# Four gate buffers, gates kept in one piece per group, the last routing among the shared experts, and the last norm in two halves

## The reference

```python
x = layernorm(x + attention(x))            # 16 heads of 8 features
xf = x.reshape(-1, 128)                    # 2048 tokens
shared = (silu(xf @ sw1) * (xf @ sw3)) @ sw2          # hidden size 256
s = sigmoid(xf @ router_w.T)                          # 8 experts
_, topk_idx = top_k(s + router_bias, 2)
gates = s_sel / (s_sel.sum() + 1e-9)                  # comb: (tokens, 8), zero where not picked
h = gelu(einsum('nd,edh->neh', xf, ew1))              # every expert on every token
routed = einsum('ned,ne->nd', einsum('neh,ehd->ned', h, ew2), comb)
out = layernorm(x + shared + routed)
```

## Time and profile before

| | us |
|---|---|
| median of 3 runs | 259.37 |
| lowest and highest run | 257.46, 260.01 |
| the profiled execution, its own time | 260.36 |
| its span, first to last instruction | 258.0 |
| PE busy | 225.7 (87%) |
| DVE busy | 169.1 (66%) |
| ACT busy | 136.0 (53%) |
| POOL busy | 92.6 (36%) |

### The profile page before, as it was taken

One profiled execution on the slowest core, in us unless ns is written; L12 is line 12 of the kernel. 1 busy time (PEld: TensorE's weight loads), 2 busy tenths in 40 slices (PEclk: granted clock), 3 DMA queues, 4 the chain that ended last, 5 costly groups with the idle time before them and its releaser, 6 DMA issues.

```text
span 258.0 us, 4343 instructions
## 1 busy us (share of the span) xinstructions
PE 225.7 (87%) x1514; PEld 153.3 (59%) x1514; DVE 169.1 (66%) x352; ACT 136.0 (53%) x260; POOL 92.6 (36%) x172
## 2 busy tenths in 40 slices
PE   1975973999999999996599999999789999999970
PEld 1533843767767776774467766648566665666630
DVE  8953992777978979797239983136646564562853
ACT  2351711676776667665146678886585334434320
POOL 8678381000100106221236976543525632020201
PEclk9997996899999999999759999999999999999997
DMA  7277764404729074285100000009995089396111
GB/s 194 55 92 93 82 68 104 43 9 79 57 44 83 14 91 39 54 76 198 38 0 0 8 0 9 1 23 158 140 225 113 21 155 146 88 148 140 41 41 41
DMA packets 16196, 19.41 MB, mean 75 GB/s; under 512 B 1280, under 2 KB 11712, under 8 KB 16032
## 3 DMA queue, kind: packets, MB, share of 16 engines
q1 hardware_dynamic: 15744, 18.49, 43.6%
q0 software_dynamic: 144, 0.39, 1.0%
q10 hardware_dynamic: 288, 0.27, 0.5%
HBM read 11.22 MB, written 1.11 MB: 48 GB/s over the span
## 4 chain that ended last, share of the span: by engine, by line
PE 78%; DMA 7%; DVE 7%; issue 3%; ACT 1%; POOL 1%; SPq 1%; POOLq 0%; DVEq 0%
PE ring L811 18%; PE pv_bank L825 14%; PE max_bank L797 12%; PE max_bank L935 11%; DMA qstack<-top_rows 5%; DVE kstack L621 3%; PE ring L781 3%; PE ring L783 2%; PE ring L782 2%; DMA kstack<-qk_parts 2%; PE max_bank L783 2%; PE max_bank L781 2%; PE max_bank L782 2%; PE misc_bank L864 1%; PE misc_bank L875 1%
## 5 line engine op out<-in xcount | busy, mean ns | idle before, releaser
L661 DVE TENSOR_REDUCE top<-max_bank 128x2 f32<-128x512 f32 x128 | 84.0, 685 | 34.0 <-PE max_bank L797 32.8
L563 ACT ACTIVATE probs_mem<-ring 128x512 f32<-128x512 f32 x128 | 73.9, 597 | 45.6 <-PE ring L811 44.3
L811 PE MATMUL ring<-qstack,kstack 128*128 128x256 f32 x256 | 63.0, 331 | 9.7 <-DMA qstack<-top_rows 9.7
L811 PEld LDWEIGHTS ring<-qstack,kstack 128*128 128x128 f32 x256 | 40.6, 199 | 37.9 <-ACT probs_mem L563 25.1
L797 PE MATMUL max_bank<-kstack,qstack 128*128 128x256 f32 x256 | 55.3, 305 | 3.8 <-DMA kstack<-qk_parts 3.0
L797 PEld LDWEIGHTS max_bank<-kstack,qstack 128*128 128x128 f32 x256 | 41.9, 203 | 7.9 <-DMA kstack<-qk_parts 3.8
L825 PE MATMUL pv_bank<-probs_mem,v 128*18 128x256 f32 x512 | 41.3, 397 | 0.0
L732 DVE TENSOR_TENSOR probs_mem<-probs_mem,kstack 128x512 f32<-128x512 f32 x32 | 22.0, 691 | 22.9 <-ACT probs_mem L601 17.4
L935 PE MATMUL max_bank<-probs_mem,wf 128*128 128x512 f32 x64 | 32.4, 593 | 0.0
L601 ACT ACTIVATE probs_mem<-ring 128x512 f32<-128x512 f32 x21 | 12.5, 596 | 20.9 <-PE ring L783 19.3
L470 POOL TENSOR_SCALAR rstd<-mv 128x2 f32<-128x2 f32 x8 | 1.8, 224 | 51.1 <-DVE mv L698 51.0
(11 more groups left out here) (139 smaller groups left out, 336.3 us busy)
## 6 DMA issues: line engine op xcount, KB each, us to landing
kstack<-gate_scratch SPq DMA_DIRECT2D x4, 2048.0 KB, 15.8
kstack<-qk_parts SPq DMA_DIRECT2D x24, 64.0 KB
wf<-w_ffn_dram SPq DMA_DIRECT2D x1, 1408.0 KB, 5.7
qstack<-qk_parts SPq DMA_DIRECT2D x9, 128.0 KB
xs<-x_dram SPq DMA_DIRECT2D x4, 256.0 KB, 4.8
out_dram<-xs SPq DMA_DIRECT2D x4, 256.0 KB, 2.3
kstack<-wf_hi SPq DMA_DIRECT2D x12, 64.0 KB
qstack<-wf_hi SPq DMA_DIRECT2D x6, 128.0 KB
```

Of the source, the lines that this page charges most:

```text
L563: nc.scalar.activation(probs[:, k // 2 % 4, c % 2 * 512:(c % 2 + 1) * 512], ring[k % NRING][:, :], ACT.Exp, scale=SCALE).then_inc(probs_ma ...
L661: dve.tensor_reduce(top[:, half, h:h + 3:2], max_bank[n % NMAX][:, :].rearrange("p (h k) -> p h k", h=2), AX.X, ALU.max).then_inc(max_take ...
L811: ins = mm(ring[k % NRING][:, j * S:(j + 1) * S], kstack[:, s, ab, r, kt * P:(kt + 1) * P], qstack[:, s, r, :], start=True, stop=True)
```

## The change

Four edits. The gates of a group lie in one piece in device memory, and a load takes 16 KB in one run for each partition in place of eight runs of 2 KB. There are four gate buffers, the two new ones in the memory of `qstack`, which the attention no longer needs by then; the loads are placed at ticks `UP0` + 1, 2, 6 and 14, and that of group 2 or 3 waits for no expert any more. The router of group 3 stands at tick `UP0` + 6 in place of `EX0` = `UP0` + 8, and the steps behind it come one half tick apart in place of two; the gate transposes of group 2 stand at `UP0` + 4 in place of `EX0` + 1, those of group 3 at `UP0` + 13 (= `EX0` + 5) in place of `EX0` + 16. The end of the last group is done in two halves of 256 tokens, the second half's transposes in a bank of their own.

```diff
-        gate_dram = nc.dram_tensor("gate_scratch", (NE, TOK), F32, kind="Internal").ap()
+        gate_dram = nc.dram_tensor("gate_scratch", (NG, NE, GT), F32, kind="Internal").ap()
...
-        gates = [kstack[:, 2 + i, :, :, :].rearrange("p a r q -> p (a r q)").rearrange("p (e t) -> p e t", e=NE).bitcast(F32)
-                 for i in range(2)]
+        gates = [kstack[:, 2 + i, :, :, :].rearrange("p a r q -> p (a r q)").bitcast(F32) for i in range(2)]
+        gates += [qstack[:, 2 * i:2 * i + 2, :, :].rearrange("p s r q -> p (s r q)").bitcast(F32) for i in range(2)]
...
-            router = 2 * EX0 if late else 2 * first + (9 if b < 2 else 8)
+            router = 2 * (UP0 + 6) if late else 2 * first + (9 if b < 2 else 8)
...
-                    n = router + n * (2 if late else 1)
+                    n = router + n
...
-                comb_tick = {NG - 1: EX0 + 16, NG - 2: EX0 + 1}.get(b // 2, router // 2 + 7)
+                comb_tick = {NG - 1: UP0 + 13, NG - 2: UP0 + 4}.get(b // 2, router // 2 + 7)
...
+        FIN = [(g, 0, TPG) for g in range(NG - 1)] + [(NG - 1, t, t + TPG // 2) for t in (0, TPG // 2)]
         for g in range(NG):
-            jobs[max(UP0 + 1, EX0 + NE * (g - 1)), 1].append(("load gates", g))
+            jobs[UP0 + (1, 2, 6, 14)[g], 1].append(("load gates", g))
...
                 for kind, i in (("accT", 0), ("finT", 1), ("rstd2", 2), ("norm2", 7)):
-                    jobs[EX0 + m + LAG + 1 + i, 0].append((kind, g))
+                    for f, (group, t0, t1) in enumerate(FIN):
+                        if group == g:
+                            jobs[EX0 + m + LAG + 1 + i, 0].append((kind, f))
...
-                if g < 2:
-                    sp.wait_ge(scores_made, 4 * NSTEP)
-                else:
-                    sp.wait_ge(hid_made, NG * NSH + NE * (g - 1))
+                sp.wait_ge(scores_made, 4 * NSTEP)
                 for i in range(2):
                     sp.wait_ge(gate_stored[i], 16 * (g + 1))
-                src = gate_dram.rearrange("(o e) t -> o e t", o=1)[:, :, tokens(g)]
-                sp.dma_start(gates[g % 2], src.to_broadcast([P, NE, GT])).then_inc(gates_loaded[g % 2], 16)
+                src = gate_dram.rearrange("(o g) e t -> o g (e t)", o=1)[:, g, :]
+                sp.dma_start(gates[g], src.to_broadcast([P, NE * GT])).then_inc(gates_loaded[g], 16)
...
-                            dve.wait_ge(gates_loaded[m // NE % 2], 16 * (m // NE // 2 + 1))
+                            dve.wait_ge(gates_loaded[m // NE], 16)
...
                     if kind == "finT":
+                        g, t0, t1 = FIN[b]
                         pe.wait_ge(acc_taken, b + 1)
-                        if b:
-                            pe.wait_ge(fin_stats, b)
-                        for t in range(TPG):
-                            ins = nc.tensor.transpose(pv_bank[:, t * P:(t + 1) * P], acc_t[:, t * P:(t + 1) * P], ident[:, :])
+                        if g and t0 == 0:
+                            pe.wait_ge(fin_stats, g)
+                        for t in range(t0, t1):
+                            ins = nc.tensor.transpose(fin_bank(b)[:, t * P:(t + 1) * P], acc_t[:, t * P:(t + 1) * P], ident[:, :])
                         ins.then_inc(fin_made, 1)
```

More of the change, by code:

```diff
@@ L179, in build_layer @@
         route_dve, route_pool = sem("route_dve"), sem("route_pool")
-        gate_stored, gates_loaded = (
-            [sem(f"{n}{i}") for i in range(2)] for n in ("gate_stored", "gates_loaded"))
+        gate_stored = [sem(f"gate_stored{i}") for i in range(2)]
+        gates_loaded = [sem(f"gates_loaded{g}") for g in range(NG)]
         rw_split, w_hi_made, w_split = sem("rw_split"), sem("w_hi_made"), sem("w_split")
@@ L747, in _ @@
                     if kind == "norm2":
+                        g, t0, t1 = FIN[b]
                         dve.wait_ge(fin_rstd, b + 1)
[L749 to L750 removed]
+                        for t in range(t0, t1):
+                            ins = dve.tensor_scalar(xs[:, g * TPG + t, :], res2[:, t, :], mv2[:, t, 0:1],
                                                     rstd2[:, t:t + 1], ALU.subtract, ALU.mult)
```

43 lines of the change are left out of this document (25 added, 18 removed).

## The result

The median of four runs of the kernel after is 264.44 us (263.81 to 265.03), against 259.69 us (257.46 to 261.88) for four runs of the kernel before. The ratio is 1.0212, with a 95% interval of 1.0138 to 1.0285. Each ratio here leaves out the runs that count as slow, over 1.5% above the fastest of their kernel (above: 261.88), so it is not the ratio of the two medians, and routing_only, with one run left, has none. The profiled execution took 265.03 us, and its span is 263.3 us; before it was 260.36 and 258.0.

A forecast was written before the change was run, and what follows sets the result against it. From 195 us on, every TensorE instruction and every wait it feels lengthens the run. The terms +5.9 - 0.52 - 0.25 - 0.6 = +4.5 against the median 259.37 gave 263.9 us; 8-in-10 range 260.9 to 268.

The forecast's parts named there:

- First wait: TensorE waits ahead of expert 1 for VectorE's product of shared part 7, queued behind `sig`: +1.96 us.
- The chain: Group 3's routing on GpSimd, from `sel` to the last comparison: 6.9 us, 5.2 plus four VectorE instructions at 0.42.
- short enough: Rival: GpSimd runs at its free durations beside idle VectorE, gates there at 202.4, sum +2.2, 261.6 us; chance 0.2.
- Last steps: Group 3's routing behind `rank`: `mask` and `picked` 0.71 us, `den` to GpSimd's last steps 0.69, those 2.25; gates at 204.65.
- All three waits together: Product of expert 3 starts at 205.8 us, before at 199.96: +5.9, including the wait ahead of expert 1.
- the second: VectorE idles at `rank` until GpSimd's comparisons end at 200.5 us; the product of expert 2 comes only at 201.7.
- the third: TensorE waits 2 to 3 us at group 3's gate transposes, until 204.7, for GpSimd's last step.
- The clock: Rival: TensorE's granted clock falls at the new gaps; total 267.2 us if at the first, 268.4 at the last; chance 0.14.
- Groups 1 and 2: Expert stage: group 3's gate transposes leave group 1, -0.52 us; the gate-load wait goes, -0.25; both groups of equal length.
- Transposes of group 2: Gate transposes moved ahead of shared part 4, into TensorE's wait for VectorE: cost nothing, at most 0.3 us.
- Last norm: End of the last group in halves: -0.45 us, half-size store 0 to 0.4, in all -0.6, bounds -0.3 and -1.1.

The follow-up runs named there:

- routing_only: The kernel before with only the moved routing and gate transposes; 265.98 us, beside 260.27 for before on that chip.
- after_again: The kernel after, unchanged, measured once more beside more runs of the kernel before; 264.26 us, ratio to before 1.0249.
- clock_fill: The kernel after with products of no use in TensorE's two long gaps, ahead of expert 1 and group 3's gate transposes; 262.79 us, ratio to before 1.0131.
- last_wait_late: The kernel after with only group 3's gate transposes three ticks later, and their load behind them; 261.68 us, ratio to before 1.0136.
- first_wait_only: The kernel after, router still early, but steps from `rank` on and group 3's gate transposes as late as before; 260.29 us, ratio to before 0.9974.
- piece_only: The kernel before with only the one-piece layout of the gates in device memory, still two buffers; 260.38 us, ratio to before 1.0045.
- routing_back: The kernel after with group 3's routing and gate transposes back at their old places; 256.87 us, ratio to before 0.9869.
- back_fill: routing_back with five products of no use ahead of the shift waits of sequences 0 and 4, bank wait moved ahead of them; 251.95 us, ratio to before 0.9648.
- back_whole_norm: routing_back with the last norm undivided; 258.43 us, ratio to before 0.9983.

## Why the prediction was right, and where its sizes were off

Forecast were +4.5 us, from 259.37 to 263.9; measured were +4.75, from 259.69 to 264.44, and +4.67 between the profiled executions. The mechanism of the waits was right. That the sums agree so closely is luck: in the stretch that the change touches it cost +6.23, 1.7 more than forecast, mainly because the clock fell, and the forecast had that at nothing. It had named a fall between 191 and 205 us as a sign of being wrong, and by that sign it was. Stages that the change does not touch (-0.93) and the time outside the span (-0.63) brought the total back, and by the medians taken beside after_again it is only +3.2. Point by point, counted from the anchor:

- *First wait.* Forecast +1.7 at `down` of expert 0 (197.0 in place of 195.29). Measured +1.74 in clock_fill and +1.74 in routing_only. Table loads, the low part of shared part 5 on POOL, `sig`, and the product of shared part 7 follow one another as the prediction put it, and `sig` is there 8.71 after the anchor (forecast 8.68). ScalarE's exponential starts 187.80, the load started 186.51 and took 1.28: the drain of some 1380 ns that the Trainium skill has on "ScalarE: Activation LUTs", section on what ACT_TABLE_LOAD costs, does not appear, so the 2.8 us that it would have added did not come.
- *The chain.* Forecast 6.9 from `sel` to the last comparison, measured 6.85. The Trainium skill, "SBUF — State Buffer", section on who interferes with whom, lets VectorE instructions with two SBUF inputs hold up GpSimd. The rows agree with it in kind: the first comparison (four instructions, L493) took 2.38 us, beside three such instructions of DVE and the start of a fourth, and 1.04 us in group 2, where DVE was idle:

```profile
163.76 1.04 POOL L485 TENSOR_TENSOR diff<-sel 128x64 f32<-128x64 f32 x4
```

  The next step, beside the rest of the fourth, took 1.19 us in place of 0.86. Behind it DVE idles, and the last three steps take 0.85, 1.15 and 0.74 us, in group 2 0.86, 1.16 and 0.73. The excess of the first two is 1.67 us, the 4 x 0.42 of the forecast. That DVE's work is what stretched them was not isolated by a run of its own. The rival *short enough* (gates at 202.4) is refuted: the chain took 6.85 in place of 5.2.
- *Last steps.* From the end of `rank` to that of `picked` 1.09, forecast 0.71; from `den_ok` to the end 2.43, forecast 2.25. `mask` took 0.66 us; the product of expert 2 runs beside it on DVE. The prediction had this only as a bound ("`mask` held up by the product of expert 2"). The gates are there 204.22 - 183.53 = 20.69 after the anchor, forecast 204.65 - 184.46 = 20.19.
- *All three waits together.* Forecast +5.9 at `down` of expert 3, the first wait in it, measured +6.4 with the clock held (clock_fill). The 0.5 are those of the last steps. Separately, the second is 1.28 at the product behind `rank`, the third 2.60 at the transposes (last_wait_late removes only the latter).
- *The clock.* This is the step that failed. The forecast had no fall; the rival gave it 0.14, with a total of 267.2 or 268.4. It fell twice, behind 3.01 us ahead of expert 1 and behind 2.60 us ahead of the transposes, and cost 1.6 to 1.7 us (clock_fill against after: 1.65 by the first medians, 1.60 anchored, 1.70 at expert 4). So the rival came true in kind, and its size was wrong: I took the 9 us of low clock at 126 to 135 as the length of a fall, and each of these lasted some 3 us. The first of them cost nothing, since its 1.4 us ended in the wait for POOL's chain; where that wait is taken away, in first_wait_only, they count.
- *Groups 1 and 2.* `down` of the first expert of groups 1 to 3 starts so:

```profile
216.31 1.02 PE L948 MATMUL max_bank<-probs_mem,wf 128*128 128x512 f32 x2
...
230.58 1.02 PE L948 MATMUL max_bank<-probs_mem,wf 128*128 128x512 f32 x2
...
244.84 1.02 PE L948 MATMUL max_bank<-probs_mem,wf 128*128 128x512 f32 x2
```

  14.27 and 14.26 us, of equal length as forecast (before 14.70 and 14.43). From expert 4's product to the last one it is 0.71 less than before; forecast 0.52 + 0.25 = 0.77. "I give the one-piece layout nothing" beside "the gate buffers no longer wait for each other: -0.25" put the right gain to the wrong edit: piece_only shows that the layout alone brings it, and routing_only that the earlier transposes alone do.
- *Transposes of group 2.* Costed at nothing ahead of shared part 4, and nothing is what they show: before, PE waits 0.51 us for DVE there, and in the kernel after part 4 starts 2.81 us ahead of the anchor, before 2.80. What their leaving brings is seen at the start of the expert stage in routing_back, where `down` of expert 0 comes 0.57 us earlier than before; in the kernel after it is inside the +1.74.
- *Last norm.* Forecast -0.6 (bounds -0.3 and -1.1), measured -1.06 to -1.18 within the span and about -0.5 outside it. The step that was off is "1.02 us for each half": POOL's power of two columns takes 0.70, and the store's gain was put at 0 to 0.4. The norm ends 260.91 - 255.79 = 5.12 us after the last product, forecast 5.5.

The sum of what was measured: 6.42 (waits) + 1.70 (clock) - 0.71 (groups) - 1.18 (end) = +6.23 within the stretch. With -0.63 outside the span and -0.93 from unchanged stages, whose length differs between executions, that makes +4.67. Against the forecast the clock is +1.7 and the last steps +0.5; the end is -0.6 and the time outside the span -0.6, and the stages ahead -0.9.

The sign hung on whether PE has enough other work while the moved routing runs, and there the forecast was right. A tick of the shared experts is six products of 0.23 us, some 1.4 us, and one of the experts 1.55, where the routing of earlier groups had ticks of some 4 us. The kernel routing_back shows that the rest of the change alone is faster than before, by 1.81 us anchored and 1.3% by its ratio.

## What to carry to other kernels

Moving a serial chain of small steps earlier pays only if the stage it moves into is long enough to cover it; count the chain's length (here some 12 us from `sig` to the gates) against the consumer's distance in the new order, and count every in-order queue that now stands behind one of its steps. Change one thing at a time where several edits are independent: here three edits worth -1.8 us together were hidden by a fourth of some +8 us. And try products of no use in a gap of TensorE that cannot be avoided: in clock_fill and at sequence 0 of back_fill the wait took about as long as before, but what followed it ran at the full clock. Find the place of the gap by counting, in the trace, the instructions ahead of it: in back_fill the second five products missed theirs by one sequence.

## What the runs showed of the hardware that was not expected

- The granted clock is not decided by the length of one gap alone. It fell behind 0.65 us of idle time in piece_only (0.57 in 192 to 196 us), and did not fall behind 3.01 us in last_wait_late (1.00 in 192 to 200 us) and in routing_only, where it then fell behind the next gap, of 2.62 us. The kernels after (both times) and first_wait_only fell behind the same 3.01. The kernel before kept 1.00 behind the same 0.65 us. What decides between them stays open; all fell to half clock for about 3 us, where the earlier trace rows show some 9. The Trainium skill, "TensorE: Matmul & The Clock Gate", section on the clock gate, has it that an idle engine falls to half clock, and that the moment of a switch varies from run to run of the same kernel. The falls agree with the first, and the one gap of 3.01 us with and without a fall behind it with the second.
- The time of an unchanged kernel goes with its granted clock. Among the 23 executions of before on the chip of after_again, the shortest (256.57 us) has a mean granted clock of 0.966, and those with 0.929 to 0.931 took 260.59 to 261.83.
- Five products of no use at the wait of sequence 0 and five ahead of sequence 4 brought 4.9 us (256.87 to 251.95, on two chips; ratios 0.9869 and 0.9648, each to its own runs of before), more than the rest of the change had to give.
- A broadcast load of 2 MB took 15.8 us from issue to landing in runs of 2 KB, and 7.5 us in runs of 16 KB.
- POOL's power of 128 x 4 numbers takes 1.02 us, of 128 x 2 numbers 0.70: half the columns take less time even at this size, but not half.
- With a last store half as large the time outside the span was 0.5 us shorter as well (2.25 in back_whole_norm, 1.76 in routing_back).
